# Attention without a loop, in eight equal slots, with numerators and denominators from one product

## The chip, the cores and the metric

One core of a Trainium2 chip. The metric is the device time of one execution of the whole program in microseconds (us). The program is two layers (attention, mixture of experts, a Mamba mixer with a Fourier network, a second mixture of experts); this change touches the first layer's attention alone.

## The reference

The touched part, for 32 batches of 256 times (T) and 128 channels (D), 16 heads of 8 channels:

```
h   = layernorm(x) * (1 + scale) + shift
ck, cv = h @ w_dk + b_dk, h @ w_dv + b_dv
q   = rope(h)                      # per head
k   = rope(ck @ w_uk + b_uk)
v   = cv @ w_uv + b_uv
p   = softmax(q k^T / sqrt(8))     # 256 x 256 per head and batch
y   = (p v, heads side by side) @ w_o + b_o
x   = x + gate * y
```

The gate, scale and shift are rows of a small product of the conditioning input; biases are zero in the data but are computed.

## The kernel before, in words

`attention(core)` (from L253) writes one program per engine; the engines meet at counting semaphores. Batch b passes through a pipeline of turns. In turn i an engine works at several batches at once: batch i at the projections, batch i-2 (MAX) at the row maxima of its scores, batch i-3 (SCORES) at scores and exponentials, batch i-4 (LAG) at the output. `rolled` (L236) emits the first six turns written out, then a hardware loop with four turns in its body that runs six times, then the last turns written out.

What one batch needs, in order:

- DVE normalises it (`xn`, L435), PE transposes and projects it (L555 to L570), ACT and DVE copy results out of the shared PSUM bank `PP`, POOL and DVE apply the rotary angles (L361, L462, L465).
- Queries and keys are split into three bf16 parts (L404, L473, L406, L483; the last of them, on DVE, is part 2). All three lie in `parts`.
- The SP queue stores `parts` to memory (L332), waits for that, and reads it back with 18 DMAs of 64 KB (L339, L340) into `Q9` and `K9`, so that one bf16 product over 72 rows gives the scores to full precision. There are four `Q9`/`K9` pairs (RING).
- PE makes the scores of each head with times of the query on partitions (L531, `MX`, two buffers), and DVE takes their row maxima (L451), head by head.
- PE transposes the maxima (L581); DVE splits them in two bf16 rows (L478, L480); SP puts these as two more rows into `Q9` (L329).
- PE makes the scores again, transposed and with the maximum taken off (L547, `ST`), ACT takes exponentials over pairs of heads (L384, `PT`).
- PE multiplies them by V, and, in a second product of the same size, by padded ones (L510): `O` holds numerators in one half and denominators in the other. DVE takes a reciprocal over 128x256 (L441) and multiplies (L444); PE applies `w_o` (L590); DVE adds the bias (L470); POOL applies the gate and adds to the residual `X` (L368, L372); DVE takes the statistics for the next layer norm (L215).

The order of the SP queue in one turn: wait for the landing of batch i-1's loads and pass that on to PE through `batch_loaded` (L319, L320); gate row of batch i-4 (L323); wait for the maxima of batch i-2 and issue their two rows (L329); wait for part 2 of batch i, store (L332); wait for the store (L43); 18 loads.

The order of PE in one turn is by eight pairs of heads. `MAXHEADS = (2, 4, 0, 4, 2, 4, 0, 0)` says how many heads of maxima stand at each pair, and value products stand at pairs 1, 3, 5, 7 only.

Of the kernel before, what the change touches and what calls it, by code (L numbers as in the profile page):

```python
# [13 lines left out]
P = 128  # L14
# [4 lines left out]
ALU = mybir.AluOpType  # L19
# [204 lines left out]
HQ = 4  # L224
PARTS = 3
KROWS = PARTS * PARTS * DH
RING = 4
PAIRS = H // 2
MAXHEADS = (2, 4, 0, 4, 2, 4, 0, 0)
MAXFROM = [sum(MAXHEADS[:p]) for p in range(PAIRS)]  # L230

# [21 lines left out]
def attention(core):  # L253
    nc, B, X, aps = core.nc, core.B, core.X, core.aps
    SCALE = float(DH) ** -0.5
    live = lambda i, lag: not isinstance(i, int) or 0 <= i - lag < B


    MAX, SCORES, LAG = 2, 3, 4
    on = ExitStack()  # L260
    with on:
# [16 lines left out]
        V = [sb(f"V_{n}", [P, TC, HQ, HQ, 32]) for n in range(RING)]  # L278
        ones = sb("ones_pad", [P, HQ, 32])
        mx = sb("row_max", [P, H, TC])  # L280
        mhi, mlo = sb("max_hi", [2 * H, P], BF16), sb("max_lo", [2 * H, P], BF16)
        PT = sb("probs", [P, 4, 2, TC, T])
        rden, oT = sb("rden", [P, T]), sb("oT", [P, T])
# [10 lines left out]
            "w_loaded", "const_ready", "mrow_const", "bo_ps", "bo_row", "bo_ready", "gate_loaded", "xn_ready", "hT_ps", "hT_ready", "ckv_ps",  # L294
            "ckv_ready", "kv_ps", "k_ready", "v_ready", "rot_ps", "cos_done", "sin_done", "roped_ready", "part0",
            "left1", "part1", "part2", "stored", "loaded", "batch_loaded", "max_ps", "max_done", "maxT_ps", "max_hi", "max_lo",
            "max_rows", "scores_ps", "exp_done", "av_done", "rden_ready", "oT_ready", "y_ps", "y_biased",
            "y_gated", "x_updated", "stats", "passed")}

        with nc.Block() as block:  # L300
            @block.sync
            def _(sp):
                for t, n in ((w_dk, "L0_attn_w_dk"), (w_dv, "L0_attn_w_dv"), (w_uk, "L0_attn_w_uk"), (w_uv, "L0_attn_w_uv"),
                             (w_o, "L0_attn_w_o"), (rot, "rope_rot")):
                    sp.dma_start(t[:], aps[n]).then_inc(S["w_loaded"], 16)
                for k, n in enumerate(("L0_attn_b_dk", "L0_attn_b_dv", "L0_attn_b_uk", "L0_attn_b_uv")):
                    sp.dma_start(bias[:, k:k + 1], aps[n].rearrange("(p n) -> p n", n=1)).then_inc(S["w_loaded"], 16)
# [9 lines left out]
                def emit(i, u):  # L317
# [3 lines left out]
                    if live(i, LAG):  # L321
                        at(sp, S["y_gated"], i - LAG)
                        sp.dma_start(ga[:], core.modrow[0, ds(i - LAG, 1), :].rearrange("n d -> (n d)").partition_broadcast(P)).then_inc(S["gate_loaded"], 16)  # L323
                    if live(i, MAX):
                        n = (u - MAX) % RING
                        at_alone(sp, S["max_lo"], i - MAX + 1, S["passed"])
                        at(sp, S["scores_ps"], PAIRS * (i - MAX - RING + 1))
                        for k, m in enumerate((mhi, mlo)):
                            sp.dma_start(Q9[n][KROWS + k:KROWS + k + 1, :, :], m[:]).then_inc(S["max_rows"], 16)  # L329
                    if live(i, 0):  # L330
                        sp.wait_ge(S["part2"], i + 1)
                        sp.dma_start(split[u], parts[:]).then_inc(S["stored"], 16)  # L332
                        at_alone(sp, S["stored"], 16 * (i + 1), S["passed"])
                        at(sp, S["scores_ps"], PAIRS * (i - RING + 1))
                        view = split[u].rearrange("(h e) a w t -> a w e h t", e=DH)
                        for a in range(PARTS):
                            for b in range(PARTS):
                                row = (a * PARTS + b) * DH
                                sp.dma_start(Q9[u][row:row + DH, :, :], view[a, 0]).then_inc(S["loaded"], 16)  # L339
                                sp.dma_start(K9[u][row:row + DH, :, :], view[b, 1]).then_inc(S["loaded"], 16)  # L340
                rolled(sp, B, LAG, 6, emit)

            @block.gpsimd
            def _(pool):
                nc.gpsimd.memset(ones[:], 0.0)
                for n in range(RING):
                    last = nc.gpsimd.memset(V[n][:], 0.0)
                last.then_inc(S["bo_row"], 1)
                pool.wait_ge(S["bo_row"], 1)
                for r in range(HQ):  # L350
                    nc.gpsimd.memset(ones[:, r, r * DH:(r + 1) * DH], 1.0)
# [5 lines left out]
                def emit(i, u):  # L357
                    if live(i, 0):
                        pool.wait_ge(S["k_ready"], i + 1)
                        at(pool, S["roped_ready"], i)  # L360
                        nc.gpsimd.tensor_tensor(qcos[:], qk[:].rearrange("p a t -> p (a t)"), cos[:], ALU.mult).then_inc(S["cos_done"], 1)  # L361
                    if live(i, LAG):
                        b = i - LAG
# [7 lines left out]
                        x = X[:, ds(b * (TC * D), TC * D)]  # L371
                        nc.gpsimd.tensor_tensor(x, x, y2[:], ALU.add).then_inc(S["x_updated"], 1)  # L372
                rolled(pool, B, LAG, 6, emit)

            @block.scalar
            def _(act):
                act.wait_ge(S["w_loaded"], 15 * 16)

                def emit(i, u):
                    for p in range(PAIRS):  # L380
                        if live(i, SCORES):
                            act.wait_ge(S["scores_ps"], PAIRS * (i - SCORES) + p + 1)
                            at(act, S["av_done"], 4 * (i - SCORES) + p // 2 - 1)
                            nc.scalar.activation(PT[:, p % 4].rearrange("p a b t -> p (a b t)"), ST[:, p % 2].rearrange("p a b t -> p (a b t)"),  # L384
                                                 ACT.Exp, scale=SCALE).then_inc(S["exp_done"], 1)
                        if p == 1 and live(i, 0):
                            act.wait_ge(S["hT_ps"], i + 1)
                            at(act, S["rot_ps"], i)
                            at(act, S["cos_done"], i)
                            nc.scalar.activation(qk[:, 0, :], PP[:, 0:T], ACT.Identity, scale=core.modcol(0, SCALE_A, i),  # L390
                                                 bias=core.modcol(0, SHIFT_A, i)).then_inc(S["hT_ready"], 1)
                        if p == 2 and live(i, 0):
                            act.wait_ge(S["ckv_ps"], i + 1)
                            at(act, S["kv_ps"], i)
                            for k in range(2):
                                last = nc.scalar.activation(ckv[:, k, :], PP[:, k * T:(k + 1) * T], ACT.Identity, bias=bias[:, k:k + 1])
                            last.then_inc(S["ckv_ready"], 1)
                        if p == 3 and live(i, 0):
                            act.wait_ge(S["v_ready"], i + 1)
                            nc.scalar.activation(qk[:, 1, :], PP[:, 0:T], ACT.Identity, bias=bias[:, 2:3]).then_inc(S["k_ready"], 1)  # L400
                        if p == 6 and live(i, 0):
                            act.wait_ge(S["roped_ready"], i + 1)
                            at(act, S["stored"], 16 * i)
                            nc.scalar.activation(parts[:, 0].rearrange("p a t -> p (a t)"), roped[:], ACT.Copy).then_inc(S["part0"], 1)  # L404
                            act.wait_ge(S["left1"], i + 1)
                            nc.scalar.activation(parts[:, 1].rearrange("p a t -> p (a t)"), left[:], ACT.Copy).then_inc(S["part1"], 1)  # L406
                rolled(act, B, LAG, 6, emit)

            @block.vector
            def _(dve):  # L410

                dve.wait_ge(S["bo_ps"], 1)
                nc.vector.tensor_tensor(bo_row[:], PP[0:1, 0:D], bo_in[:], ALU.add).then_inc(S["bo_ready"], 1)
# [13 lines left out]
                def emit(i, u):  # L427
                    for p in range(PAIRS):
                        if p == 1 and live(i, LAG + 1):
                            new_stats(i - LAG - 1)  # L430
                        if p == 0 and live(i, 0):
                            at(dve, S["hT_ps"], i)
                            for k in range(TC):
                                c = 2 * i + k
# [10 lines left out]
                        if live(i, MAX):  # L445
                            b = i - MAX
                            for h in range(MAXFROM[p], MAXFROM[p] + MAXHEADS[p]):
                                dve.wait_ge(S["max_ps"], H * b + h + 1)
                                if h == 0:
                                    at(dve, S["maxT_ps"], b)  # L450
# [39 lines left out]
            def _(pe):  # L490
# [9 lines left out]
                def values(b, u, g, k):  # L500

                    if k == 0:
                        pe.wait_ge(S["exp_done"], PAIRS * b + 2 * g + 2)
                        if g == 0:
                            at(pe, S["oT_ready"], b)
# [1803 lines left out]
```

## Time and profile before

| | |
|---|---|
| median of 3 runs | 4135.03 us (4131.96 to 4137.02) |
| profiled execution | 4145.38 us, span 4143.6 us |
| PE, DVE, ACT, POOL busy, share of the span | 71%, 72%, 47%, 50% |
| mean granted clock of PE | 0.827 of full |
| attention | from about 53 to 998 us |

The profile is of one execution. A busy time is the union of the instructions of an engine. "Idle before, releaser" of an instruction names what ended the engine's wait. SPq is the queue of SyncE, on which DMAs are issued; L43 is the line of a helper that waits. The granted clock is the share of TensorE's 2.4 GHz that it was given; 0.50 is 1.2 GHz.

### The profile page before, as it was taken

How to read it: one execution, taken by the hardware profiler on the slowest of the kernel's cores; microseconds unless marked ns; L12 is line 12 of the kernel's file. 1: busy time of each engine (PE TensorE's matmuls, PEld its weight loads, DVE VectorE, ACT ScalarE, POOL GpSimd, SP SyncE). 2: the span in 40 equal slices, each digit the busy share in tenths (PEclk: the TensorE clock that was granted, in tenths of full speed). 3: DMA queues.
4: the chain of work that ended last, by engine and by line, in shares of the span. 5: the costliest groups of instructions: out<-in, count | busy, mean ns of one | idle time of the engine just before them, and what ended most of it. 6: DMA issues, size and time to landing. Idle time of an engine off the chain costs nothing. (4 is left out here: it accounts for less than half of the span.)

```text
span 4143.6 us, 59984 instructions
## 1 busy us (share of the span) xinstructions
PE 2949.8 (71%) x18442; PEld 2001.6 (48%) x18443; DVE 2980.8 (72%) x4269; ACT 1930.7 (47%) x3012; POOL 2068.5 (50%) x1342
## 2 busy tenths in 40 slices
PE   3788878776329999127777777777777777649954
PEld 2444444443316666014555545555555554539954
DVE  3566656555714444647999999999999999957744
ACT  1343334334213333017766666676777767322223
POOL 0010001011752222119888888888888888702226
PEclk9988888887569999568788888888888888669965
DMA  4545555554211111513333333333233233210041
GB/s 84 62 64 57 61 58 60 60 60 100 77 46 39 39 39 37 160 30 88 77 81 82 81 81 80 79 81 80 77 80 80 77 81 81 70 69 23 23 134 24
DMA packets 274682, 285.94 MB, mean 69 GB/s; under 512 B 34892, under 2 KB 186470, under 8 KB 274202
## 3 DMA queue, kind: packets, MB, share of 16 engines
q1 hardware_dynamic: 262210, 264.41, 31.5%
q0 software_dynamic: 12256, 18.82, 1.3%
q8 instruction: 116, 1.90, 0.2%
q14 instruction: 100, 0.82, 0.1%
HBM read 236.57 MB, written 54.22 MB: 70 GB/s over the span
## 5 line engine op out<-in xcount | busy, mean ns | idle before, releaser
L1645 POOL TENSOR_TENSOR resid_x<-s_ux,s_B_rows 128x1024 f32<-128x1024 f32 x512 | 1204.1, 2357 | 213.6 <-PE s_y L1892 212.7
L1838 DVE TENSOR_TENSOR_SCAN resid_x<-s_dA,resid_x 128x1024 f32<-128x1024 f32 x512 | 1167.1, 2280 | 79.1 <-ACT s_dA L1706 76.1
L1706 ACT ACTIVATE s_dA<-s_dt,s_A 128x510 f32<-128x510 f32 x1024 | 661.9, 678 | 425.5 <-DVE resid_x L1838 423.4
L1892 PE MATMUL s_y<-identity,resid_x 128*128 128x128 f32 x4096 | 652.7, 312 | 0.0
L1892 PEld LDWEIGHTS s_y<-identity,resid_x 128*128 128x128 f32 x4096 | 586.8, 164 | 98.3 <-issue 68.5
L1846 DVE TENSOR_TENSOR resid_x<-resid_x,s_C 128x1024 f32<-128x1024 f32 x512 | 611.2, 1194 | 6.9 <-PE s_C L1882 6.7
L1882 PE MATMUL s_C<-s_bc_parts,s_w_sel 96*128 96x512 bf16 x512 | 229.8, 449 | 401.7 <-DVE resid_x L1846 399.5
L451 DVE TENSOR_REDUCE a_row_max<-a_maxscores 128x2 f32<-128x512 f32 x512 | 328.4, 683 | 217.9 <-PE a_maxscores L531 217.3
L384 ACT ACTIVATE a_probs<-a_scores 128x1024 f32<-128x1024 f32 x256 | 260.6, 1021 | 374.3 <-PE a_scores L547 371.7
L1882 PEld LDWEIGHTS s_C<-s_bc_parts,s_w_sel 96*128 96x128 bf16 x512 | 51.2, 100 | 598.0 <-DVE resid_x L1846 566.4
L1177 POOL DMA_INDIRECT choice_outputs<-e_y,e_idx x135 | 130.9, 970 | 338.4 <-DVE e_y L1162 338.1
L1915 PE MATMUL s_prep<-s_xT,s_w_taps 128*128 128x512 f32 x512 | 264.8, 643 | 8.1 <-ACT s_dt L1734 5.3
L361 POOL TENSOR_TENSOR a_qk_cos<-a_qk,a_cos 128x512 f32<-128x512 f32 x32 | 40.6, 1267 | 453.8 <-ACT a_qk L400 453.8
L1168 DVE TENSOR_TENSOR e_g<-e_silu,e_ps 128x512 f32<-128x512 f32 x135 | 92.8, 688 | 220.8 <-ACT e_silu L1146 166.9
L531 PE MATMUL a_maxscores<-a_K,a_Q 72*128 72x256 bf16 x1024 | 183.4, 307 | 87.2 <-SPq L320 78.3
L547 PE MATMUL a_scores<-a_Q,a_K 74*128 74x256 bf16 x1024 | 178.8, 304 | 81.2 <-DMA a_Q<-a_max_lo 81.0
L2208 PE MATMUL k_psY<-k_coef_T,k_basis 128*128 128x128 f32 x2048 | 233.3, 276 | 0.0
L2208 PEld LDWEIGHTS k_psY<-k_coef_T,k_basis 128*128 128x128 f32 x2048 | 232.1, 193 | 0.0
L368 POOL TENSOR_TENSOR a_y<-a_y,a_gate_rows 128x256 f32<-128x256 f32 x32 | 23.4, 730 | 404.3 <-DMA a_gate_rows<-mod_rows 322.2
L1141 ACT ACTIVATE e_gT<-e_psG 128x512 f32<-128x512 f32 x135 | 80.6, 597 | 250.5 <-PE e_psG L1116 250.5
L510 PE MATMUL a_out<-a_probs,a_V 128*32 128x256 f32 x2048 | 178.1, 422 | 7.5 <-DVE a_oT L444 4.6
L531 PEld LDWEIGHTS a_maxscores<-a_K,a_Q 72*128 72x128 bf16 x1024 | 99.6, 109 | 170.6 <-issue 70.7
(315 smaller groups left out, 5212.2 us busy)
## 6 DMA issues: line engine op xcount, KB each, us to landing
s_B_rows<-b_rows SPq DMA_DIRECT2D x256, 512.0 KB, 4.9
a_Q<-split_qk SPq DMA_DIRECT2D x288, 64.0 KB
a_K<-split_qk SPq DMA_DIRECT2D x288, 64.0 KB
split_qk<-a_parts SPq DMA_DIRECT2D x32, 384.0 KB, 2.5
e_x<-slot_inputs SPq DMA_DIRECT2D x135, 65.0 KB, 1.8
f_mod_rows<-mod_rows SPq DMA_DIRECT2D x16, 512.0 KB, 7.6
c_y<-choice_outputs SPq DMA_DIRECT2D x16, 512.0 KB, 6.8
e_w<-L_ffn_w SPq DMA_DIRECT2D x3, 2048.0 KB, 15.6
```

The costliest lines, as they stand in the source:

```text
L384: nc.scalar.activation(PT[:, p % 4].rearrange("p a b t -> p (a b t)"), ST[:, p % 2].rearrange("p a b t -> p (a b t)"), ACT.Exp, scale=SCAL ...
L451: nc.vector.tensor_reduce(mx[:, h, :], MX[:, h % 2], AX.X, ALU.max).then_inc(S["max_done"], 1)
L531: last = mm(MX[:, h % 2, k, :], Q9[n][0:KROWS, h, k * P:(k + 1) * P], K9[n][0:KROWS, h, :], start=True, stop=True)
L547: last = mm(ST[:, p % 2, j, k, :], K9[n][:, h, k * P:(k + 1) * P], Q9[n][:, h, :], start=True, stop=True)
L1645: tt(R[:, s % 4, d], ux[par][:, d], bsb[s % BRING][:, d].unsqueeze(1).broadcast_to([P, C2, W]), ALU.mult).then_inc(S["in_ready"], 1)
L1706: last = func(dA[:, d, c2, :, lo:lo + T - 1], dt[par][:, d, c2, :].rearrange("p (g t) -> p g t", t=T)[:, :, lo:lo + T - 1], ACT.Exp, scale ...
L1838: nc.vector.tensor_tensor_scan(r, a, r, 0.0, ALU.mult, ALU.add).then_inc(S["scanned"], 1)
L1846: tt(r, r, CP[:].unsqueeze(1).broadcast_to([P, C2, W]), ALU.mult).then_inc(S["part_ready"], 1)
L1882: mm(CP[:], Wt["sel"][:, (c % DIRS) * DS + c // DIRS, :], bcs[par][:], start=True, stop=True).then_inc(S["C_ps"], 1)
L1892: last = mm(YP[:, t, c2 * P:(c2 + 1) * P], R[:, s % 4, d, c2, t * P:(t + 1) * P], core.ident[:], is_transpose=True, start=(c == 0 and t % ...
L1915: last = mm(PR[:], Wt["taps"][:, d, c, k, :], xT[:, :, off:off + T], start=(k == 0), stop=(k == DC - 1))
L2208: last = nc.tensor.matmul(psY[:, n, k * D:(k + 1) * D], basis[n][:, m, k * P:(k + 1) * P], WT[:, m, :], start=(m == 0), stop=(m == NBASIS ...
```

## The change

The attention is written out for all 32 + 6 turns; its loop goes. The stages of a batch are spread over more turns: projections in turn i, store and loads in turn i+1 (before: in turn i), row maxima in i+2, the maxima's rows in i+3, scores in i+3 (last three slots) and i+4, values in i+3 (last slot) and i+4, division and output product in i+5, gate and statistics in i+6. PE's turn becomes eight equal slots: two heads of maxima, one pair of scores, half a value product.

SP doesn't wait for landings; each of the four buffers has its own semaphore, on which PE waits. The order of the SP queue becomes: part 2 of batch i-1, store; rows of the maxima of batch i-3; wait for the store; 18 loads; gate row. On DVE part 2 of a batch stands behind the row maxima of heads 0 and 1 of the next turn.

Numerators and denominators come from one product: in V each head takes 16 columns of a group of 32, eight for values and one set to 1.0. ACT copies `O` to SBUF, PE transposes it (four transposes) so that time lies on partitions, DVE takes a reciprocal over 128x32 and multiplies (128x256), PE transposes back (two), ACT copies to `oT`. The V copies go from DVE to ACT. The rows of `w_o` and `b_uv` come in another order. `mx` has two buffers, V five.

```diff
 # SP, one turn
-                    if live(i, 1):
-                        sp.wait_ge(S["loaded"], 16 * 2 * PARTS * PARTS * i)
-                        sp.sem_inc(S["batch_loaded"], 1)
...
+                for i in range(B + LAST):
+                    if live(i, 1):
+                        b = i - 1
+                        at(sp, S["scores_ps"], PAIRS * (b - RING + 1))
+                        sp.wait_ge(S["part2"], b + 1)
+                        sp.dma_start(split[b % RING], parts[:]).then_inc(S["stored"], 16)
+                    if live(i, ROWS):
+                        b = i - ROWS
+                        sp.wait_ge(S["max_lo"], b + 1)
+                        for k, m in enumerate((mhi, mlo)):
+                            sp.dma_start(Q9[b % RING][KROWS + k:KROWS + k + 1, :, :], m[:]).then_inc(S["max_rows"], 16)
+                    if live(i, 1):
+                        b = i - 1
+                        n = b % RING
+                        sp.wait_ge(S["stored"], 16 * (b + 1))
...
+                                sp.dma_start(Q9[n][row:row + DH, :, :], view[a, 0]).then_inc(loaded[n], 16)
+                                sp.dma_start(K9[n][row:row + DH, :, :], view[c, 1]).then_inc(loaded[n], 16)
+                    if live(i, OUT):
...
 # DVE, start of a turn
+                for i in range(B + LAST + 1):
+                    if live(i, LAST):
...
+                        tt(y1[:], PP[:, 0:TC * D], bo[:], ALU.add).then_inc(S["y_biased"], 1)
+                    row_max(i, 0)
+                    if live(i, 0):
...
+                        last.then_inc(S["xn_ready"], 1)
+                    row_max(i, 1)
+                    if live(i, 1):
+                        dve.wait_ge(S["part1"], i)
+                        tt(parts[:, 2].rearrange("p a t -> p (a t)"), left[:], parts[:, 1].rearrange("p a t -> p (a t)"),
+                           ALU.subtract).then_inc(S["part2"], 1)
+                    if live(i, ROWS):
+                        b = i - ROWS
+                        dve.wait_ge(S["maxT_ps"], b + 1)
...
+                    for h in range(2, 8):
+                        row_max(i, h)
...
 # PE
+                        if h == 0:
+                            pe.wait_ge(loaded[n], 16 * 2 * PARTS * PARTS * (b // RING + 1))
...
+                        for q in range(HQ):
+                            last = mm(O[32 * q:32 * q + 32, g // 2, :], V[b % VRING][:, k, q, g, :], PT[:, (2 * g + q // 2) % 4, q % 2, k, :],
+                                      start=(half == 0), stop=(half == PAIRS - 1), skip_group_check=True)
...
+                def slot(i, p):
+                    max_scores(i, 2 * p)
+                    scores(i, p)
+                    max_scores(i, 2 * p + 1)
+                    values(i, p)
+
+                for i in range(B + LAST):
+                    slot(i, 0)
+                    if live(i, ROWS):
+                        b = i - ROWS
+                        pe.wait_ge(S["max_done"], H * (b + 1))
...
+                        nc.tensor.transpose(PP[0:2 * H, 0:P], mx[b % 2][:].rearrange("p h k -> p (h k)"), core.ident[:]).then_inc(S["maxT_ps"], 1)
+                    slot(i, 1)
...
```

## Rows read from the trace of the kernel before

**Rows 1.** Busy time of each engine over the attention's loop; first line the columns.

```profile
...
core 0: us, PE busy (x) PEld busy (x) DVE busy (x) ACT busy (x) POOL busy (x), PEclk, DMA share, GB/s
60.00:951.00 891.00, 699.26 (x6347) 386.19 (x6345) 527.39 (x955) 335.66 (x430) 81.24 (x88) 0.88 0.52 60
...
```

**Rows 2.** Waits of the SP queue, 60 to 1000 us: us in total, times, longest us.

```profile
...
SPq L320 <- DMA a_K<-split_qk: 322.0, 32, 12.0
SPq L43 <- DMA split_qk<-a_parts: 46.8, 24, 2.7
...
```

**Rows 3.** Timeline of the SP queue over one turn: start us, us, what is issued.

```profile
...
591.68 0.50 SPq L332 DMA_DIRECT2D split_qk<-a_parts  x1
594.33 0.29 SPq L339 DMA_DIRECT2D a_Q<-split_qk  x1
...
618.23 0.37 SPq L323 DMA_DIRECT2D a_gate_rows<-mod_rows  x1
...
619.98 0.52 SPq L332 DMA_DIRECT2D split_qk<-a_parts  x1
```

**Rows 4.** One line of the program (L332): duration ns min/median/max, first and last start us.

```profile
...
L332 SPq DMA_DIRECT2D split_qk<-a_parts x32: 337/514/585, 68.1 to 927.3; - x32
...
```

**Rows 5.** Timeline of the SP queue in two early turns and in the last.

```profile
...
93.47 0.35 SPq L332 DMA_DIRECT2D split_qk<-a_parts  x1
95.82 0.27 SPq L339 DMA_DIRECT2D a_Q<-split_qk  x1
...
118.79 0.60 SPq L329 DMA_DIRECT2D a_Q<-a_max_hi  x1
...
120.06 0.58 SPq L332 DMA_DIRECT2D split_qk<-a_parts  x1
...
927.31 0.58 SPq L332 DMA_DIRECT2D split_qk<-a_parts  x1
929.87 0.29 SPq L339 DMA_DIRECT2D a_Q<-split_qk  x1
...
```

**Rows 6.** Stretches of one microsecond, columns as in Rows 1.

```profile
...
561.00:562.00 1.00, 0.00 (x0) 0.00 (x0) 0.00 (x0) 0.00 (x0) 0.00 (x0) 0.58 0.00 0
605.00:606.00 1.00, 1.00 (x17) 0.42 (x16) 1.00 (x2) 0.00 (x0) 0.00 (x0) 1.00 0.65 61
616.00:617.00 1.00, 0.00 (x0) 0.00 (x0) 1.00 (x3) 0.20 (x1) 0.00 (x0) 1.00 0.08 5
...
```

**Rows 7.** Waits of the engines, 60 to 1000 us, columns as in Rows 2.

```profile
...
PE a_maxscores L531 <- SPq L320: 78.3, 27, 15.3
```

**Rows 8.** Timeline of DVE about one turn's end.

```profile
...
614.85 0.28 DVE L480 TENSOR_TENSOR a_max_lo<-a_proj,a_max_hi 32x128 bf16<-32x128 f32 x1
...
616.27 0.68 DVE L483 TENSOR_TENSOR a_parts<-a_left,a_parts 128x512 bf16<-128x512 f32 x1
616.87 0.60 DVE L435 TENSOR_SCALAR a_xn<-resid_x,rstd,neg_mean_rstd 128x128 f32 x2
618.58 1.29 DVE L451 TENSOR_REDUCE a_row_max<-a_maxscores 128x2 f32<-128x512 f32 x2 [1.11 <-PE a_maxscores L531]
...
```

**Rows 9.** Timeline of PE and DVE around the last batch's landing, and the stage's end.

```profile
...
951.59 1.03 PE L531 MATMUL a_maxscores<-a_K,a_Q 72*128 72x256 bf16 x4 [3.71 <-SPq L320]
...
952.23 1.29 DVE L451 TENSOR_REDUCE a_row_max<-a_maxscores 128x2 f32<-128x512 f32 x2 [3.90 <-PE a_maxscores L531]
...
998.10 1.28 ACT L210 ACT_TABLE_LOAD   x1 [9.71 <-PEq L300]
...
```

**Rows 10.** Groups of instructions, 200 to 800 us: busy us, mean ns, idle before.

```profile
...
L510 PE MATMUL a_out<-a_probs,a_ones_pad 128*32 128x256 f32 x1368 | 116.3, 413 | 0.0
...
L555 PE MATMUL a_proj<-identity,a_xn 128*128 128x128 f32 x44 | 13.5, 404 | 0.0
...
```

**Rows 11.** Timeline of POOL ahead of the loop.

```profile
...
39.28 3.62 POOL L347 MEMSET a_V<- 128x1024 f32 x4
...
```

**Rows 12.** Timeline of PE at the start of a turn of the loop.

```profile
...
533.46 0.69 PE L531 MATMUL a_maxscores<-a_K,a_Q 72*128 72x256 bf16 x4 [3.36 <-issue]
```

More of the change, by code:

```diff
@@ L227 @@
 RING = 4
+VRING = 5
 PAIRS = H // 2
-MAXHEADS = (2, 4, 0, 4, 2, 4, 0, 0)
-MAXFROM = [sum(MAXHEADS[:p]) for p in range(PAIRS)]
 def pair_heads(p):
@@ L343, in _ @@
+                    if live(i, OUT):
+                        b = i - OUT
+                        at(sp, S["y_gated"], b)
+                        sp.dma_start(ga[:], core.modrow[0, b:b + 1, :].rearrange("n d -> (n d)").partition_broadcast(P)).then_inc(S["gate_loaded"], 16)
             @block.gpsimd
             def _(pool):
-                nc.gpsimd.memset(ones[:], 0.0)
-                for n in range(RING):
+                for n in range(VRING):
                     last = nc.gpsimd.memset(V[n][:], 0.0)
-                last.then_inc(S["bo_row"], 1)
@@ L349, in _ @@
-                pool.wait_ge(S["bo_row"], 1)
-                for r in range(HQ):
-                    nc.gpsimd.memset(ones[:, r, r * DH:(r + 1) * DH], 1.0)
+                last.then_inc(S["v_zero"], 1)
+                pool.wait_ge(S["v_zero"], 1)
+                for n in range(VRING):
+                    for c in range(2):
+                        nc.gpsimd.memset(V[n][:].rearrange("p k q (a c) m -> p (k q a) c m", c=2)[:, :, c, 16 * c + DH:16 * c + DH + 1], 1.0)
                 nc.gpsimd.memset(minus[:], -1.0)
@@ L377, in _ @@
                 act.wait_ge(S["w_loaded"], 15 * 16)
[L379 to L406, printed above, removed]
@@ L592, in _, with scores @@
[L592 removed]
+                def scores(i, p):
+                    q, lag = scored(p)
+                    if live(i, lag):
+                        b = i - lag
+                        n = b % RING
+                        if q == 0:
+                            pe.wait_ge(S["max_rows"], 32 * (b + 1))
+                        at(pe, S["exp_done"], PAIRS * b + q - 1)
+                        for j, h in enumerate(pair_heads(q)):
+                            for k in range(TC):
+                                last = mm(ST[:, q % 2, j, k, :], K9[n][:, h, k * P:(k + 1) * P], Q9[n][:, h, :], start=True, stop=True)
+                        last.then_inc(S["scores_ps"], 1)
@@ L2300 @@
     arrays["L1_ffn_b1_cols"] = np.ascontiguousarray(arrays.pop("L1_ffn_b1").reshape(E * FC, P).T)
+    order = np.arange(D).reshape(HQ, 2, 2, DH).transpose(1, 0, 2, 3).ravel()
+    for n in ("L0_attn_w_o", "L0_attn_b_uv"):
+        arrays[n + "_by_group"] = np.ascontiguousarray(arrays.pop(n)[order])
     arrays["x_tiles"] = x.reshape(B * TC, P, D)
```

383 lines of the change are left out of this document (198 added, 185 removed).

## The prediction

> **What bounds the kernel now.** I read the busy times of the attention stage first [rows 1]. Nothing is full: in 891 us PE is busy 699, DVE 527, ACT 336, and the DMA engines 0.52 of the time. A stage in which everything has room is set by a chain, so the next view is the SP queue's waits [rows 2]: in every one of 32 batches it stands at L320 for the landing of that batch's loads, 322.0 us or 10.1 us each, and that is counted from the last load's issue. It hardly waits for anything else.
>
> One turn of the queue then reads as a closed ring [rows 3]: store of the parts at 591.68, first of the 18 loads at 594.33 (2.65 us, since the loads read back what was stored), landing at about 618.2 where the gate issue follows L320, next store at 619.98. The turn is 28.3 us. Over all batches it is (927.3 - 68.1) / 31 = 27.7 us [rows 4]. Taking the same three pieces over all 32 batches of the timeline, first and last of which are shown in part [rows 5], I get as means: store to first load 2.63, first load to landing 23.0, landing to next store 2.07; their sum is 27.7. While the loads run the DMA share stands flat at 0.65, and when they end it is 0.08 [rows 6]: 23 of 27.7 us are one transfer that nothing overlaps. PE in turn waits 78.3 us for that landing in 27 waits [rows 7].
>
> **What the change does to the ring.** SP no longer waits for the landing (L320 and the relay semaphore go); PE waits for the loads itself. That looks like freedom for SP, but the ring closes in another way. DVE runs in the order written: row maxima of heads 0 and 1 of turn i (batch i-2), and only behind them part 2 of batch i-1. SP can't store batch i-1 before part 2, nor load it before the store. The maxima need batch i-2 to have landed. So the loads of one batch still start only after those of the batch before have landed, and now PE and DVE work stands between. In the old code part 2 was done by then: it ends 616.95, the landing is at 618.2 [rows 3, 8]. The old link from landing to store was only SP's own issuing (gate, two rows).
>
> New link, landing to store. PE has been idle for long and is at half clock: in a gap of this kind the granted clock is already down to 0.58 in the second microsecond [rows 6], and at the last landing four of these matmuls take 1.03 us and the first maximum starts 952.23 - 951.59 = 0.65 us after PE [rows 9]. Then two maxima, 1.29 us together, the two normalisations between them, 0.60, and part 2, 0.68 [rows 8]: 0.65 + 1.29 + 0.60 + 0.68 = 3.2, and with the signal to SP 3.25 us, against 2.07. That is +1.2 us. Below, 2.9 (the instructions overlap a little, PE in full clock); above, 3.9, should head 1's matmuls, which at half clock stand behind four score matmuls, hold DVE for 0.7 us.
>
> Store to first load. The two row DMAs now stand behind the store instead of in front. Without them in front it took 95.82 - 93.47 = 2.35 us [rows 5] against 2.63: -0.3 us. But SP now waits for the row maxima's low part between the store and the loads. PE gets there after 8 bf16 matmuls (two times 1.03 at half clock [rows 9]), four value products and a transpose, about 3.4 us from the landing by my estimate; then two DVE instructions of 0.28 [rows 8] make 4.0, and two issues of 0.6 each [rows 5] 5.2. The store lands at 3.25 + 2.3 = 5.55. So this wait is hidden, by 0.3 us. If PE is a microsecond later, it costs 0.7 us a batch. Range -0.3 to +0.5, I take -0.3.
>
> Loads themselves: same 18 DMAs, same sizes. 23.0 us, mean unchanged; the single batches scatter by some microseconds, and I allow 0.4 us for the mean.
>
> New turn: 23.0 + 3.25 + 2.35 = 28.6 us, against 27.7. Over 31 turns: 31 x 0.9 = +28 us.
>
> **What comes off PE, DVE and moves to ACT.** Half of the value matmuls go: those against the padded ones are 116.3 us in the 600 us window, 21.7 turns, so -5.4 us a turn; six transposes come, at 13.5 / 44 = 0.31 us each +1.8 [rows 10]. PE goes from 699.3 / 891 x 27.7 = 21.7 to about 18 us busy a turn [rows 1]. DVE has 16.4 us, loses the reciprocal over 256 columns (now 32) and the V copies and gets nothing larger; ACT has 10.4 and gets four copies, even at 1 us each 14.4. All lie under 28.6, with PE, the nearest, having some 9 us of cover. So I cost all of it at nothing inside the ring: a shorter product makes PE wait longer for the landing. Without that cover the 3.6 us would be worth 31 x 3.6 = 112 us. The separate wait of PE for the row DMAs goes too, under the same cover. The moved gate DMA (64 KB) is issued right behind the loads; as it is last in the queue I take 0, and up to +0.5 us a turn if it takes its share while they run.
>
> **Start and end.** POOL clears five V buffers of 0.9 us for four [rows 11] and writes more small ones, ahead of the constants' release: +1 us. End: from the last landing to the next stage it is 998.1 - 951.6 = 46.5 us [rows 9]. There PE and ACT do set the time. I lay out the new turns as 17 (last maxima), 9, 8, 4 and 3 us (last output, then gate and statistics) = 41: -5 us, with -10 and +3 as ends.
>
> **The sum.** +28 + 1 - 5 = +24 us. The profiled execution took 4145.4 us (span 4143.6), so such a run would take 4169; the median of the runs is 4135.0, 10 us less, and there the sum gives 4159.
>
> **No loop.** A turn of the loop begins with PE idle for 3.36 us and nothing shown that it waits for [rows 12]. There are six such turns; were each on the path, taking them out would give at most 6 x 3.4 = 20 us. I count 0, since SP's ring and not PE sets the pace. The Trainium skill (Runtime: NRT & Kernel Launch, Instruction fetch mechanics) says that a taken branch to a page outside the window costs a fetch, while straight code is streamed ahead; by that rule alone the long straight code costs nothing and the loop's end gains those 20 us. The PE row agrees with a stall, but doesn't show the fetch.
>
> **Rivals.**
> 1. No measurable change, 4137 us. The straight code makes every hop as short as in the first turns, which were already written out: landing to store was 1.3 us there [rows 5] against 2.07, and the loads ran 0.4 us faster. If that holds for the new link too, the turn is 0.8 us shorter than I have it, 27.8: 31 x 0.1 + 1 - 5 = 0, and the PE stalls of [rows 12] decide the last microseconds. For it: those turns took 26.3 us. Against: they had no gate and partly no rows to issue, which explains most.
> 2. Faster, 4060 us. The mechanism is that SP isn't held by the landing: part 2 is there before it, store and next loads queue up behind the running ones. Place: the link landing to store, which falls to nothing; the turn is 23.0 + 2.35 = 25.3 us, -2.4 x 31 = -74. It decides from the point at which a store is issued while loads are still in flight. Against: DVE's written order excludes it, as far as I can read it. Work alone (PE 18 us) would even allow more.
> 3. Clearly slower, 4195 us. PE is late with the transposed maxima (+0.7) and the gate's transfer mixes with the loads' end (+0.5): 31 x 1.2 = +37 on top of mine.
>
> **Chances and range.** Mine 0.62, rival 1 0.14, rival 2 0.10, rival 3 0.14. Mine reaches by its bounds (2.9 to 3.9 for the link, 0.4 for the loads, the ends) from 4130 to 4190. The range of 8 in 10 is 4127 to 4195: rival 2 and the far end of rival 3 stay out. What can be told from no change is 0.2%, 8 us. Faster than that: 0.10 for rival 2, and 0.06 of the low edges. Within: 0.14. Slower: 0.70.
>
> **What would show it.** Right: after the change stores follow each other every 28.6 us; each store comes 0.1 us after part 2 of DVE, and 3.2 us after the first matmul of the maxima; PE's wait for the loads grows from 78 us to over 200 in the stage; the first load follows the store by 2.35 us; DMA share at 0.65 in plateaus with a gap of 7 to 8 us. Wrong: a store issued with loads in flight or no gap in the plateaus (rival 2); SP waiting longest for the row maxima (rival 3); loads of a batch other than 23 us, which no step here foresees and which at 31 turns weighs most.

## The result and the profile after

The changed kernel takes 4195.55 us (median of 4 runs, 4190.71 to 4218.14) against 4136.02 for the kernel before in the same comparison: ratio 1.0128, interval 1.0096 to 1.016. It is slower, by 59.5 us where 24 was forecast. The time stands at the upper edge of the range, which ended at 4195.

The profiled execution took 4197.6 us (span 4195.5), 52 us more than that of before. Both are one execution each, and all of the difference lies in the attention, whose end (the table load of ScalarE that closes [rows 9]) moved from 998.1 to 1051.1 us. From the page of the changed kernel, the span in 40 slices:

```profile
...
PE   3687787878409999407777777777777777649954
...
PEclk6677777775559999758788888888888888669965
...
DMA  3554555542511111432233333333333333210041
```

The attention is slices 1 to 10. PE is not full in them, and its granted clock is 0.6 to 0.7, falling to 0.5 at the end; the mean clock of the whole program is 0.78 against 0.827. The kernel before had this clock over the same slices:

```profile
...
PEclk9988888887569999568788888888888888669965
```

Over all but the end of the attention, in the columns of [rows 1]:

```profile
60.00:984.00 924.00, 710.42 (x4545) 379.72 (x4545) 479.19 (x883) 367.00 (x546) 79.86 (x86) 0.71 0.51 58
```

The granted clock is 0.71 where it was 0.88 [rows 1]. So PE is busy 710.4 us in these 924, or 22.2 us a turn, although half of the value products are gone; before it was 21.7.

Where the 53 us are, by the line that stores a batch's parts (L326 now, L332 in [rows 4]); duration ns min/median/max, first and last start:

```profile
L326 SPq DMA_DIRECT2D split_qk<-a_parts x32: 342/343/346, 68.5 to 962.4; - x32
```

Start +0.4 us. Between the first and the last store lie (962.4 - 68.5) / 31 = 28.84 us a turn against 27.72: 31 x 1.12 = +34.7. From the last store to the stage's end 88.7 against 70.8: +17.9. Sum +53.0.

The waits changed places as the ring says (landing, maxima, part 2, store, next loads, landing). First SP's own, 60 to 1051 us; us in total, times, longest:

```profile
SPq L325 <- DVE a_parts L484: 346.6, 28, 14.6
SPq L326 <- DVE a_parts L484: 57.8, 4, 18.6
SPq L331 <- DVE a_max_lo L492: 36.6, 5, 22.7
SPq L340 <- DMA split_qk<-a_parts: 26.8, 32, 3.3
...
```

Then those of the engines in the same stretch:

```profile
...
DVE a_row_max L465 <- PE a_maxscores L544: 395.5, 216, 15.1
...
PE a_maxscores L544 <- DMA a_K<-split_qk: 193.3, 32, 16.1
```

SP doesn't wait for the landing any more [rows 2]; it waits 404 us for part 2 (L484), and PE waits for the landing instead: 193.3 us, where it was 78.3 [rows 7]. The wait for the row maxima's low part, rival 3, is 36.6 us in 5 turns, 22.7 of them in one turn behind the last loads: hidden in the 27 others.

One landing and the next store, from the timeline of the changed kernel (start us, us, engine, line; in brackets the idle time before and what ended it):

```profile
...
557.45 0.34 SPq L326 DMA_DIRECT2D split_qk<-a_parts  x1
...
559.82 0.29 SPq L340 DMA_DIRECT2D a_Q<-split_qk  x1
...
560.81 1.06 PE L557 MATMUL a_scores<-a_Q,a_K 74*128 74x256 bf16 x4
...
563.24 1.22 PE L601 MATMUL a_proj<-a_qk,a_w_dk 128*128 128x256 f32 x2
...
564.26 1.06 PE L602 MATMUL a_proj<-a_qk,a_w_dv 128*128 128x256 f32 x2
...
565.54 0.63 PE L557 MATMUL a_scores<-a_Q,a_K 74*128 74x256 bf16 x4
...
577.27 0.42 DVE L472 TENSOR_TENSOR a_y<-a_proj,a_bias_out 128x256 f32<-128x256 f32 x1 [0.50 <-PE a_proj L636]
...
584.11 0.61 PE L544 MATMUL a_maxscores<-a_K,a_Q 72*128 72x256 bf16 x2 [6.87 <-DMA a_K<-split_qk]
...
584.75 0.69 DVE L465 TENSOR_REDUCE a_row_max<-a_maxscores 128x2 f32<-128x512 f32 x1 [7.05 <-PE a_maxscores L544]
...
585.36 0.89 DVE L478 TENSOR_SCALAR a_xn<-resid_x,rstd,neg_mean_rstd 128x128 f32<-128x128 f32 x2
...
586.77 0.68 DVE L484 TENSOR_TENSOR a_parts<-a_left,a_parts 128x512 bf16<-128x512 f32 x1
...
587.52 0.34 SPq L326 DMA_DIRECT2D split_qk<-a_parts  x1
```

PE begins after the landing at 584.11, DVE's first maximum starts 0.64 later, part 2 stands behind two maxima and the normalisations, and the store follows 3.41 us after PE's first matmul. DVE and PE had nothing to do for 7 us before: part 2 could have been made at 577.7. Over all turns the means are store to first load 2.42 (foreseen 2.35), first load to PE's first matmul 23.0 (23.0), that matmul to the next store 3.39 (3.25).

### The profile page after: what moved, and what is told of

Same layout as the page of the kernel before. It is cut to its first block and busy times, and to the rows that moved or that the text cites. A ratio compares the mean times of both kernels' runs of the same rounds, so it can differ in the third digit from the quotient of the medians.

```text
span 4195.5 us, 54518 instructions
## 1 busy us (share of the span) xinstructions
PE 2982.8 (71%) x16586; PEld 1999.4 (48%) x16587; DVE 2931.2 (70%) x4205; ACT 1970.9 (47%) x3140; POOL 2071.5 (49%) x1348
## 5 line engine op out<-in xcount | busy, mean ns | idle before, releaser
L465 DVE TENSOR_REDUCE a_row_max<-a_maxscores 128x2 f32<-128x512 f32 x512 | 344.2, 686 | 396.2 <-PE a_maxscores L544 395.5
L544 PE MATMUL a_maxscores<-a_K,a_Q 72*128 72x256 bf16 x1024 | 257.9, 346 | 208.1 <-DMA a_K<-split_qk 193.3
L544 PEld LDWEIGHTS a_maxscores<-a_K,a_Q 72*128 72x128 bf16 x1024 | 111.3, 120 | 297.2 <-DMA a_K<-split_qk 202.0
L571 PE MATMUL a_out<-a_probs,a_V 128*32 128x256 f32 x2048 | 213.5, 498 | 0.5 <-ACT a_probs L389 0.5
L557 PE MATMUL a_scores<-a_Q,a_K 74*128 74x256 bf16 x1024 | 211.1, 344 | 0.0
```

Of the source, the lines that this page charges most:

```text
L465: nc.vector.tensor_reduce(mx[b % 2][:, h, :], MX[:, h % 2], AX.X, ALU.max).then_inc(S["max_done"], 1)
L544: last = mm(MX[:, h % 2, k, :], Q9[n][0:KROWS, h, k * P:(k + 1) * P], K9[n][0:KROWS, h, :], start=True, stop=True)
L571: last = mm(O[32 * q:32 * q + 32, g // 2, :], V[b % VRING][:, k, q, g, :], PT[:, (2 * g + q // 2) % 4, q % 2, k, :], start=(half == 0), st ...
```

## The term that was mis-sized: the end

From PE's first maxima of the last batch, at 987.6, to the stage's end it is 63.5 us. Before it was 46.5 [rows 9], and I had 41. The transfers are over by then, so it is work. Stretches of the changed kernel's end, columns as in [rows 1] (the last three: granted clock of PE, DMA share, GB/s):

```profile
992.00:997.00 5.00, 5.00 (x31) 2.00 (x30) 2.17 (x5) 2.05 (x2) 0.00 (x0) 0.50 0.06 16
...
1012.00:1017.00 5.00, 5.00 (x29) 2.30 (x29) 1.38 (x5) 1.82 (x2) 1.46 (x2) 0.50 0.00 0
...
1032.00:1037.00 5.00, 5.00 (x49) 1.84 (x48) 0.61 (x3) 3.84 (x4) 1.45 (x2) 0.88 0.06 13
```

And the same place in the kernel before:

```profile
951.00:957.00 6.00, 2.49 (x11) 1.47 (x12) 1.70 (x4) 0.39 (x1) 1.44 (x2) 0.50 0.07 18
957.00:963.00 6.00, 6.00 (x53) 3.09 (x52) 3.62 (x6) 2.19 (x3) 0.00 (x0) 0.71 0.04 9
963.00:969.00 6.00, 4.67 (x53) 2.30 (x52) 5.33 (x9) 2.43 (x3) 0.00 (x0) 1.00 0.00 0
```

Both reach the last landing at half clock. The old order is back at full clock some ten microseconds later. The new one has PE busy in all 5.00 us of each stretch from 992 to 1032 and the clock at 0.50 (1.2 GHz) from 987 on, in the stretches shown and in those between them. In 5 us PE makes about 31 matmuls there, where the old order made 53 in 6 us. The end's work was counted at full clock, and was done at half.

How much of this is the clock can be read from the kernels of the experiments, since most of them have the same end. Here first the changed kernel, then the one with part 2 first, then one with unused products added to the end, and last the kernel before, each from its last landing on (columns as above):

```profile
987.00:1050.00 63.00, 55.85 (x342) 25.49 (x342) 18.48 (x40) 24.82 (x28) 7.18 (x10) 0.58 0.02 5
...
965.00:1017.00 52.00, 44.55 (x342) 21.83 (x342) 18.95 (x42) 24.28 (x28) 7.24 (x10) 0.76 0.03 6
...
998.00:1050.00 52.00, 44.67 (x362) 24.07 (x362) 18.37 (x40) 24.28 (x28) 7.21 (x10) 0.83 0.03 7
...
951.00:997.00 46.00, 34.59 (x397) 19.16 (x397) 19.78 (x33) 15.73 (x16) 5.72 (x8) 0.87 0.03 8
```

Nine profiles of the changed kernel and its variants have an end without added products, with 341 to 343 matmuls of PE in it. It grows as the mean clock falls: 52.5 and 53.1 us at 0.76, 56.4 to 56.9 at 0.68, 60.5 at 0.64, 61.5 at 0.61, 63.5 at 0.58. The shortest end of the new order, 47.2 us at 0.94, is that of a kernel with added products (rows from ScalarE's queue, products at the end); its PE reached the last batch without a wait and was at 1.00 from 977 to 1017. By the difference of 63.5 and 47.2, some 16 of the 22 us that the forecast was short of are the clock.

## Experiments

The runs of different chips differ, so each ratio is to the kernel before on the same chip (4152.57, 4152.18, 4142.19 and 4141.37 us in the four groups below). Turns and ends are read from one profile of each kernel, and the turn of one and the same ring came out at 28.71, 28.84 and 29.10 us in three of them (the third is of the kernel that differs in the last turns only). Comments in the code cuts are put in to say what a cut is.

**Part 2 first (the ring).** If the link from landing to store is what sets the turn, DVE making part 2 ahead of the first maximum opens it.

```diff
+                    if live(i, 1):   # part 2, moved up
...
                     row_max(i, 0)
```

> The changed kernel with one move on DVE: part 2 of batch i-1 stands at the start of turn i, ahead of the row maxima, not behind those of heads 0 and 1. Ring theory (loads can start only after the landing before them, through PE, two maxima, normalisation and part 2): the 3.4 us from PE's first matmul to the next store leave the ring, the store is issued while loads are in flight, and the turn falls from 28.8 us to between 24 and 25.5 (transfer 21.5 with the gate row, store and its landing 2.4, start 0.9). 31 turns by 3.4 to 4.8 us: 105 to 150 us less, 4050 to 4090. Rival (the turn is long because PE's eight slots run at half clock for longer): no change in the turn, 4195, because PE's work isn't touched.

Measured: 4169.98 us, ratio 1.0052 (1.0032 to 1.0073); turn 27.88. A gain on the change of 0.6 to 0.8%, but a quarter of the one expected. SP's waits in this kernel, 60 to 1000 us:

```profile
SPq L331 <- DVE a_max_lo L492: 257.1, 32, 19.2
SPq L325 <- DVE a_parts L475: 148.1, 27, 8.9
```

and its timeline:

```profile
795.56 0.34 SPq L326 DMA_DIRECT2D split_qk<-a_parts  x1
...
800.16 0.61 PE L544 MATMUL a_maxscores<-a_K,a_Q 72*128 72x256 bf16 x2 [5.74 <-DMA a_K<-split_qk]
...
803.74 0.28 DVE L492 TENSOR_TENSOR a_max_lo<-a_proj,a_max_hi 32x128 bf16<-32x128 f32 x1
...
804.05 0.52 SPq L331 DMA_DIRECT2D a_Q<-a_max_hi  x1
...
804.61 0.59 SPq L331 DMA_DIRECT2D a_Q<-a_max_lo  x1
...
805.24 0.48 SPq L340 DMA_DIRECT2D a_Q<-split_qk  x1
```

The store is out 4.6 us before PE has its data; then SP stands at L331 for the split maxima, which PE and DVE make only behind the landing, and the loads are issued 5.1 us after it. The ring had a second closer, hidden just behind the first. I hadn't seen that, though the prediction had put the hidden wait at 0.3 us of distance.

**Normalisation behind part 2 (one term of the link).**

```diff
                     row_max(i, 0)
-                    if live(i, 0):   # normalisation, 0.60 us
...
                     row_max(i, 1)
                     if live(i, 1):   # part 2
```

> The changed kernel with the two normalising instructions of DVE behind part 2 and not between the maxima of heads 0 and 1. Ring theory: the link from landing to store loses at most their 0.6 us, less what DVE then waits for head 1's matmuls, which PE makes 1.25 us after head 0's; the normalisation now fills only part of that wait, so I expect the link shorter by 0.3 to 0.6 us and the total by 10 to 19 us: 4177 to 4186. Rival (PE's slots set the turn): the projections start later, so the same time or up to 10 us more.

Measured: 4194.53 us, 1.0111 (1.0085 to 1.0137). The link went from 3.39 to 3.19, the turn to 28.80: DVE now waits for PE's second head instead (0.59 us at 560.67 in its timeline). That is a miss: 10 to 19 us less were expected. PE's matmuls are as much a part of this link as DVE's work; the 0.60 of the normalisation wasn't a term of its own.

**Maxima made twice (is PE covered?).** PE makes the maxima of heads 2 to 15 a second time in the stage.

```diff
-                        for k in range(TC):
+                        for k in list(range(TC)) * (2 if h >= 2 and i < B else 1):
```

> The changed kernel with every matmul for the maxima of heads 2 to 15 made twice in the first 32 turns: 28 more matmuls of 256 columns, 3.0 us of PE a turn at full clock and up to 6 at half. Ring theory: PE waits 6 to 7 us for the landing in every turn and this is taken out of that wait; total 4195, within 10 us, the wait for the landing down from 193 us to about 90. Rival (PE's work sets the turn): 31 turns by 3.0 us, 4290 or more.

Measured: 4210.07 us, 1.0135 (1.0099 to 1.0172); the change itself has 1.0128 and, repeated, 1.0109. Between 60 and 1000 us PE is busy 773.0 us for 723.5, and its wait for the landing falls from 193.3 us, though not to the 90 expected:

```profile
PE a_maxscores L544 <- DMA a_K<-split_qk: 155.1, 30, 18.3
```

The turn is 29.47, +0.6. Some 50 us more of busy time cost at most 20: most of PE's work lies under the loads. The matmuls themselves are more work than that; the granted clock was 0.79 with them (60 to 984) and 0.71 without.

**Half of the denominators' product in the kernel before (what was the removed product worth?).**

```diff
-                    for kind in range(2):
+                    for kind in range(2 if k == 0 else 1):
```

> The kernel before, with half of the denominators' products left out (only the first half of the keys is summed in the denominators), which takes 16 of 64 value matmuls out of a turn, 1.7 us of PE at full clock. Ring theory: SP's wait for the landing sets the turn at 27.7 us and PE's work is under it, so the turn stays and only the end gains some 3 us: 4128 to 4136. Rival (PE's work counts in full): 32 by 1.7, 4080.

The kernel leaves out the denominators' sum over the second half of the keys. Measured: 4148.25 us, 0.9996 (0.9978 to 1.0014): nothing. SP's wait for the landing stands as it was:

```profile
SPq L320 <- DMA a_K<-split_qk: 320.2, 32, 11.3
```

So taking value matmuls off PE buys nothing inside a ring that waits for loads, as costed.

**Gate DMA ahead of the loads.** It is issued behind the store instead of behind the loads.

```diff
+                    if live(i, OUT):   # gate DMA, moved ahead of the maxima's rows
...
                     if live(i, ROWS):
```

> The changed kernel with the gate row's DMA (64 KB, 128 packets of 512 B) issued between the store and the rows of the maxima, not behind the 18 loads. Where it stands now it shares the engines with the loads: 2432 packets in 21.6 us, against 2304 in 20.8 before. If it costs the ring its transfer, the loads get back to 20.8 us and the turn shortens by up to 0.7 us: 28 turns, 10 to 20 us less, 4175 to 4186. Rival (the landing that PE waits for is that of the loads alone, and the gate's packets only trail behind it): same, 4195, within 6 us; 0.3 us more if the gate delays the store's landing.

Measured: 4182.49 us, 1.0068 (1.0044 to 1.0092). The turn is 28.61 against 28.84 and 28.71, which would be 3 to 7 us; the end is 56.9. That the gate's transfer costs anything where it stands isn't shown: the turn differs by no more than those of one ring do, and the interval overlaps that of the repeated change.

**Projection products in the last turns (the clock at the end).** The three turns behind the last batch get the projections' products of the other turns, unused.

```diff
+                    elif i < B + ROWS:
...
+                        mm(PP[:, 0:T], w_dk[:], qk[:, 0, :], start=True, stop=True)
+                        mm(PP[:, T:2 * T], w_dv[:], qk[:, 0, :], start=True, stop=True)
```

> The changed kernel with more work for PE: in the three turns after the last projections it makes the projections' products once more into the shared bank, and nobody reads them (five products of 256 columns, 1.7 us a turn at full clock). Clock theory of the end (63.5 us from the last landing to the next stage, because PE runs at half clock from 987 to 1032, and in the turns before it came back to full clock just as these products were made): the clock rises some 8 us after the last landing, the end shortens by 12 to 20 us, to 43 to 52, total 4175 to 4184, though PE does more. Rival (the end is long since there are more turns with more hand-overs in them): it gets longer by 5 to 10 us, 4200 to 4206.

Measured: 4192.78 us, 1.0097 (1.0071 to 1.0123). The end is 52.6 us long, though PE does more in it, against 63.5 and 56.9 in the two profiles of the change. One of its stretches:

```profile
...
1008.00:1013.00 5.00, 5.00 (x37) 3.29 (x36) 2.35 (x5) 1.16 (x2) 0.00 (x0) 0.80 0.00 0
...
```

PE starts on the last landing at 998.4 here, and the clock comes back at about 1010, 12 us later. In the median this can't be told from the change; its turn is 29.10, in a profile of 4198. Nor does a short end need the products: the kernel with part 2 first, which has none of them, reaches its last landing at 965.1, is at 1.00 again from 985 and has an end of 52.5 us. What the profiles show is that the clock comes back sooner with them: 11 to 12 us after the last landing in two kernels with the products (a third was at full clock before it), 19 to 46 us in the nine profiles without. In ordinary turns of the change it also returns where these products are made: the four score matmuls take 1.06 us at 560.81 in the timeline above, ahead of L601 and L602, and 0.63 at 565.54, behind them.

**The change once more.**

> The changed kernel once more, beside the others on their chip: ratio 1.013 to the kernel before, as in its first timing (1.0096 to 1.016), turn 28.8 us. A second profile shows how far the end of attention (63.5 us in the first) scatters by itself: the clock theory of the end allows 52 to 64, since it depends on when PE comes back to full clock.

Measured: 4190.68 us, 1.0109 (1.0084 to 1.0134); turn 28.71, end 56.9. Its clock in the end is 0.50 from 990 to 1010, 0.60 to 1020, and then 1.00. So the turn repeats, and the end scatters between profiles of the very same kernel, by 6.6 us, and with the clock.

**Both halves: part 2 first, gate early, products at the end.** The three edits above together.

> The changed kernel with three of these edits: part 2 first, gate row between store and rows, and the unused products in the last turns. Ring theory: turn 24 to 25, end 43 to 52 us: 4030 to 4070, below the kernel before (4136). With the store issued while loads are in flight, it must wait in the DMA queue for them, so SP stands 10 us or more at the store's landing in every turn; if PE, now with little idle time, stays at full clock, nothing else comes near. Rival: the gate in the queue ahead of the next loads costs what it saves, same as the first edit alone.

Measured: 4175.34 us, 1.0051 (1.0028 to 1.0073), turn 28.58, end 52.5. In the median that is the same as part 2 alone, and far from the 4030 to 4070 expected. The two turns, 28.58 and 27.88, are of profiles that took 4187 and 4162 us, one above and one below its kernel's median, so they show no loss. SP still waits for the maxima's rows ahead of the loads, and the other two edits bring nothing that can be measured.

**Rows from the queue of ScalarE.** To open the second closer, the row DMAs leave SP, so that no load stands behind them; part 2 is first.

```diff
 # ACT, behind exponentials(i, 2)
+                            act.dma_start(Q9[b % RING][KROWS + k:KROWS + k + 1, :, :], m[:]).then_inc(S["max_rows"], 16)
```

> Part 2 first, as in the first edit, and the two DMAs of the maxima's rows are issued from ACT's queue, behind its third exponential, no longer by SP between store and loads. The first edit left SP waiting 257 us (8.0 a turn) at L331 for the low part of the maxima, which needs the batch before to have landed: the ring had closed again one step later. Ring theory, second form: with both links gone SP waits only for the store's landing, which queues behind the running loads; the turn is transfer 21.5, store 2.3, start 1.0: 24.5 to 25.5 us, 31 times 2.4 to 3.4 less than the first edit's 27.9, so 75 to 105 us below it. On this chip the first edit stood at 1.005 of the kernel before: now 0.980 to 0.987. PE's own turn (22.7 us from landing to its last product) is close behind, so PE should wait only 2 to 3 us. Rival (the loads' own rate falls when store, rows and loads overlap): turn 27 or more, ratio 0.998 or above.

Measured: 4184.12 us, 1.0107 (1.0075 to 1.0138); turn 28.52. A plain miss. There is a third closer:

```profile
...
789.04 0.51 ACTq L401 DMA_DIRECT2D a_Q<-a_max_hi  x1
...
789.58 0.61 ACTq L401 DMA_DIRECT2D a_Q<-a_max_lo  x1
...
801.23 0.61 PE L557 MATMUL a_scores<-a_Q,a_K 74*128 74x256 bf16 x4 [3.63 <-DMA a_Q<-a_max_lo]
```

Two small rows, issued while the loads run, release PE 11.7 us later. Over the stage (60 to 1000) that is

```profile
PE a_scores L557 <- DMA a_Q<-a_max_lo: 100.0, 30, 5.6
```

and PE, which makes scores and maxima in one order, comes late to the next maxima. That this holds the ring is read from this one trace; no run changes it alone. By it the rows should be issued ahead of the loads. The Trainium skill (DMA: Bandwidth & Descriptors, Queues, rings and completion order) says that a DMA engine takes turns between the queues that have work for it, packet by packet. By that I would expect the rows to come through soon. The median of these DMAs, 3.2 us from issue to landing, agrees; the longest, 13.6, doesn't.

With the products at the end as well:

> The same with the unused products of the projections in the turns after the last batch. If the end again takes 52 us with them against 52 to 63 without, as in the two earlier pairs, it is 0 to 10 us below the run without them. Rival: with PE nearly without idle time it comes into the end at full clock anyway, and the products cost 3 to 5 us.

4171.62 us, 1.0092 (1.0058 to 1.0126), turn 28.23, end 47.2 against 56.4 without them; the medians' intervals overlap. And the rows alone moved, part 2 in its place:

> Only the rows' DMAs on ACT's queue; part 2 stays behind the maxima of heads 0 and 1. Ring theory: that link still holds the ring, and the rows were hidden behind the store's landing there, so the turn stays 28.8 us and the time that of the changed kernel, within 8 us. Rival (each of the two moves brings its own half): 31 by 1 to 2 us less.

4194.9 us, 1.0115 (1.0082 to 1.0147), turn 28.77: as long as part 2 closes the ring, the rows' queue is of no account.

**Everything ahead of the landing.** The last kernel makes part 2 and the maxima's rows at the start of a turn, on SP and ahead of the loads: PE transposes the maxima before its first slot, which is where it waits for the loads, and DVE splits them before its first maximum.

```diff
 # PE
+                    if live(i, ROWS):   # transpose of the maxima, moved up
...
                     slot(i, 0)
 # DVE: part 2, maxima's split, then
                     row_max(i, 0)
```

> All three closers of the ring are taken out together, with rows and loads on SP as in the changed kernel: on DVE part 2 and the split of the maxima stand ahead of the maxima of head 0, and PE transposes the maxima of the turn before ahead of its first matmuls, which wait for the landing. So part 2 and both rows are ready while the loads before are in flight; the rows go out ahead of the next 18 loads and not behind them, as they effectively did in the run with ACT's queue (issued 789.6, landed 801.2, PE waits 100 us for them). Ring theory, third form: the turn is the DMA queue's alone, transfer 21.5, then the store's landing and the first load's start, 2.4 to 3.5: 24 to 25 us; PE's own turn (22.7 us from landing to last product, plus 1.5 for the bias and the transposed maxima) stands at the same 24. 31 times 3.8 to 4.8 less than the changed kernel's 28.8: 118 to 150 us less, ratio to the kernel before 0.975 to 0.985. Rival, which now has two misses of mine behind it: something else in the turn takes the place once more (the store's landing held back by the running loads, or PE at half clock), turn 27 or more, ratio 1.00 or above.

Measured: 4092.37 us (4063.98 to 4097.72), 0.9883 (0.9861 to 0.9904). It beats both kernels, by less than expected (0.975 to 0.985). Its stores, and SP around one of them:

```profile
L326 SPq DMA_DIRECT2D split_qk<-a_parts x32: 342/343/810, 68.7 to 839.5; - x32
```

```profile
...
805.20 0.68 DVE L475 TENSOR_TENSOR a_parts<-a_left,a_parts 128x512 bf16<-128x512 f32 x1
...
805.96 0.34 SPq L326 DMA_DIRECT2D split_qk<-a_parts  x1
...
806.41 0.52 SPq L331 DMA_DIRECT2D a_Q<-a_max_hi  x1
806.97 0.59 SPq L331 DMA_DIRECT2D a_Q<-a_max_lo  x1
...
813.36 0.61 PE L544 MATMUL a_maxscores<-a_K,a_Q 72*128 72x256 bf16 x2 [7.66 <-DMA a_K<-split_qk]
...
814.44 0.29 SPq L340 DMA_DIRECT2D a_Q<-split_qk  x1
```

Store and rows are out 7 us before the landing, and the next load follows it by 1.1 us, where in the change it is 3.4 + 2.4 = 5.8. The store lands late among the running loads: SP waits 90.2 us for the stores in 32 turns, 9.2 at the longest. The turn is (839.5 - 68.7) / 31 = 24.87. This is rival 2 of the prediction. Part 2 by itself had given 0.6 to 0.8%; with the maxima's transpose and split moved too it is 2.2 to 2.4%, against the change. But the loads don't set every turn: PE waits for a landing in 20 of them (109.8 us). Turns of 19.0 us and of 27 to 34 us alternate between 709 and 840 us, and the clock goes with them (columns as in [rows 1]):

```profile
787.00:806.00 19.00, 17.38 (x151) 9.73 (x148) 15.12 (x30) 12.09 (x18) 2.45 (x3) 1.00 0.61 68
...
813.00:823.00 10.00, 9.64 (x52) 4.72 (x53) 4.86 (x8) 3.63 (x4) 1.44 (x2) 0.50 0.53 57
```

In the long turn PE waits for the landing until 813.4 and then works to 839.2, first at 0.50; the next store comes at 839.5. Behind the landing that turn is PE's own work.

The profiled execution, 4064, was the fastest of seven; why the others lie near 4090 I don't know. If the 28 us between it and the median all lay in the ring, the usual turn would be 25.8 us; no profile shows that.

## Why the prediction was right and wrong

- **The ring, right.** No store is issued with loads in flight, SP waits for part 2 and PE for the landing, and work on PE is covered (maxima twice: at most 20 of 50 us; half the denominators: 0). PE's wait for the landing was 193.3 us where over 200 was foreseen. Opening it wholly makes the kernel 1.2% faster than before.
- **New turn, 28.6: 28.84.** The loads were 23.0 as foreseen. The link was 3.39 for 3.25 and store to first load 2.42 for 2.35. The 31 turns cost +34.7 us for +28, 7 short. That the link adds up from DVE's durations was too simple (moving the normalisation's 0.60 gave back 0.2).
- **What comes off PE, wrong but without effect on the ring.** From 21.7 us busy a turn PE was to go to about 18. It went to 22.2, since the granted clock fell from 0.88 to 0.71. The cover is 6.0 us a turn of waiting for the landing, and not some 9. The forecast took PE's durations from the kernel before, at its clock, and the same assumption failed at the end.
- **Start, +1: +0.4.** Right.
- **End, -5: +17 in the profile, +10 in its repetition.** This is the term that was mis-sized. "There PE and ACT do set the time" was right; the turns laid out as 17, 9, 8, 4 and 3 us took PE's clock to return as it did in the kernel before. It stayed at half for 29 us after the last landing in one profile and for 45 in the other. The bound of +3 didn't hold it either. At a mean clock of 0.94 the new end took 47.2 us with unused products in it, which their expectation put at 1.7 us in each of three turns; that leaves 42 by my estimate, so the layout of the turns was about right and the clock was not. I knew that PE comes out of each wait at half clock and didn't ask, for the last turns, what they would take if it stayed there.
- **The sum.** In the profile +53 for +24: 7 from the turn, 22 from the end. The bounds of the forecast, added as they are listed, reach 4199 and not 4190 (20 us for the link, 12 for the loads, 8 for the end), before the bound of store to first load. Of the medians' 59.5 the rest, 7, is that of the two profiled executions: before's took 10 us more than the median of its runs, the change's 2 more.
- **Rival 3, 4195.** The time is its own, the mechanism isn't: the wait for the rows' maxima stayed hidden in nearly all turns, and issuing the gate's transfer early gave 0.1 to 0.2 us a turn in the profiles, no more than their scatter, and not 0.5.
- **Rival 2, 4060.** "DVE's written order excludes it" was right and half of the story: SP's order, and the order in which PE transposes, exclude it as well.
- **Rival 1.** A link as short as in the first turns didn't come; they lack the work that stands in it.

Left open: what brings the clock back in the end (it came back sooner with the added products, but the profiles don't show what in them does it), why the executions of the last kernel scatter by 0.8%, the cause of the loads' flat DMA share of 0.65, and what the removed loop alone is worth, which wasn't tried separately.

## What to carry to other kernels

When one transfer fills most of a turn, ask for each instruction between its landing and the next issue why it must be there, and follow every wait of the issuing queue to the work it hangs on: here three chains (part 2, the maxima's rows, and those rows' place behind loads) closed the same ring, and only opening all of them beat the old kernel, with 24.9 us a turn in its profile for 28.8. Work taken off a covered engine is worth nothing, but the run-out of the pipeline has no cover, so cost it at both clocks.

## What the runs showed of the hardware

- The granted clock can stay at 0.50 while the profile has PE busy throughout: 992 to 1032 us in one profile of the changed kernel, 990 to 1010 in another. PE had come out of a wait for the landing in both.
- With the same 341 to 343 matmuls of PE in it, the end of the attention took 52.5 us at a mean granted clock of 0.76 and 63.5 at 0.58.
- In the last kernel, a turn that begins without a wait for the landing (787 to 806) is at 1.00 throughout and takes 19.0 us; the next one begins with 7.66 us of idle PE, has 0.50 behind it, and takes 34.
- Small DMAs from another queue, issued among running 64 KB loads, took up to 13.6 us to land.
